# A kernel of attention and feed-forward: one PSUM copy between the two moved from VectorE to ScalarE

## The chip, the cores and the metric

The kernel runs on one Trainium2 chip, on all 8 of its cores. Each core computes one of eight independent batch entries with the same program; nothing is exchanged. The metric is the device time of the slowest core in microseconds. The engines are called PE (TensorE), DVE (VectorE), ACT (ScalarE), POOL (GpSimd) and SP (the one that here issues the output transfers).

## The reference

One layer with a normalisation before and after each half, on x of 8 x 2048 x 1024 (a core has 2048 x 1024):

```
def _layernorm(x, axis=-1, eps=1e-5):
    m = jnp.mean(x, axis=axis, keepdims=True)
    v = jnp.var(x, axis=axis, keepdims=True)
    return (x - m) / jnp.sqrt(v + eps)
...
    x = x + _layernorm(_L0_attn_ref(_layernorm(x, axis=-1), ...), axis=-1)
    x = x + _layernorm(_L0_ffn_ref(_layernorm(x, axis=-1), ...), axis=-1)
```

The attention has 16 heads of 64 and is causal; the feed-forward has 3072 hidden units, silu(gate) * up, with integer weights scaled by 1/127.

## The kernel before

Data lie in SBUF either token-major (128 tokens in the partitions, 1024 features along a row: a tile; there are NJ = 16 tiles) or feature-major (`s_f`, 8 blocks of 128 features by 2048 tokens). Matrix products work on the feature-major form, normalisations on the token-major one. The kernel goes through six stages one after the other: normalise x and transpose it; attention; the output projection (into `s_f`, ACT adds the bias, L750); the stage of this case; the feed-forward; and a last normalisation with the output.

The stage of this case is a software pipeline over the 16 tiles, from the projection's result to the feed-forward's input. For tile j:

- `p3_A(j)`: PE transposes the 8 blocks of the tile from `s_f` into a PSUM bank of `pO` (L762, banks alternate by j % 2); one copy brings the 1024 bf16 values of each partition into `s_ln` as `ztm` (L769, two buffers by j % 2); then `emit_ln` normalises `ztm` into `s_at`.
- `p3_B(j)`: POOL adds the result to the residual `s_x` (L781).
- `p3_C(j)`: `emit_ln` normalises the new `s_x` tile, its mean being known already.
- `p3_D(j)`: PE transposes it into another PSUM bank (L801), and ACT copies that into `s_f` (L809).

`emit_ln` is a chain over two engines: on DVE the sum (L240, left out in `p3_C`), the sum of squares (L246, which reads the tile twice and leaves its product in `s_dmp`), and two small instructions for the variance (L251, L254); on ACT Ln and Exp for the reciprocal root (L257, L260); on DVE one small instruction (L263); on ACT the normalisation itself (L266).

The loop emits step t as

```python
    for t in range(NJ + 3):
        if t < NJ:
            p3_A(t)
        if 0 <= t - 1 < NJ:
            p3_B(t - 1)
        if 0 <= t - 2 < NJ:
            p3_C(t - 2)
        if 0 <= t - 3 < NJ:
            p3_D(t - 3)
```

There is no planner and no reordering: `Prog.op` records each operation with what it reads and writes, and `emit_all` writes them to each engine's queue in the order of emission, with a semaphore wait for each operation that it depends on. An engine works through its queue in that order. So in step t ACT has, of this stage, Ln, Exp and L266 of tile t, then Ln, Exp and L266 of tile t-2, then L809 of tile t-3.

The last stage (`p6_T`, `p6_L`, `p6_AD`) has a similar pipeline, where ACT copies the transposed tile out of PSUM into `s_ln` (L917).

Of the kernel before, what the change touches and what calls it, by code (L numbers as in the profile page):

```python
# [26 lines left out]
class Prog:  # L27
# [12 lines left out]
    def op(self, engine, emit, reads=(), writes=(), queue=None, war=(),  # L40
           deps=(), bump=()):
        idx = len(self.ops)
        dep = set(deps)
        for r in reads:
            e = self.res.get(r)
            if e is not None and e[0] is not None:
                dep.add(e[0])
        for w in tuple(writes) + tuple(war):
            e = self.res.get(w)
            if e is not None:  # L50
                if e[0] is not None:
                    dep.add(e[0])
                dep |= e[1]
        dep.discard(idx)
        self.ops.append({"engine": engine, "emit": emit, "deps": dep,
                         "queue": queue, "token": None})
        for r in reads:
            self.res.setdefault(r, [None, set()])[1].add(idx)
        for w in writes:
            self.res[w] = [idx, set()]  # L60
        for w in bump:
            self.res.setdefault(w, [None, set()])[0] = idx
        return idx
# [59 lines left out]
def build_program(trunc=0, trunc_step=None):  # L123
# [40 lines left out]
    op = P.op  # L164
# [591 lines left out]
    def p3_A(j):  # L756
        par = j % 2
        bank1 = "ps%d" % (4 + par)
        pb = pO[:, 512 * par:512 * (par + 1)].bitcast(BF16)
        for c in range(ND):  # L760
            op("pe",
               lambda e, c=c, j=j, pb=pb: e.transpose(  # L762
                   pb[:, 128 * c:128 * (c + 1)],
                   s_f[:, S * c + 128 * j: S * c + 128 * (j + 1)], IDT),
               reads=["zf_%d_%d" % (c, j // 4), "cst"],
               writes=([bank1] if c == 0 else []),
               bump=([] if c == 0 else [bank1]))
        ztm = s_ln[:, 1024 * par:1024 * (par + 1)]
        op("dve", lambda e, pb=pb, ztm=ztm: e.tensor_copy(ztm, pb[:, 0:1024]),  # L769
           reads=[bank1], writes=["lnr%d" % par],  # L770
           war=["osc0", "osc1"])
        yn = s_at[:, 1024 * par:1024 * (par + 1)]
        emit_ln(ztm, "lnr%d" % par, yn, "yn%d" % par, pid=j % 4, eng="dve",
                dst_war=("at0",) if j < 2 else (),
                war0=(["rrq0", "rrq1", "onq0", "onq1"] if j == 0 else ()))
# [37 lines left out]
# [9 lines that stand above are left out]
# [169 lines left out]
```

How the kernel before makes its waits and increments, by code:

```python
        def body(ename, eng):  # L89
            wm = {}
            def wait(ch, val):
                if wm.get(ch, 0) < val:
                    eng.wait_ge(sems[ch], val)
                    wm[ch] = val
            for i in per_eng[ename]:
                o = ops[i]
                if o["queue"] is not None and i in burst_settle:
                    wait(o["queue"], burst_settle[i])
                for d in sorted(o["deps"]):
                    ch, val, _ = ops[d]["token"]
                    if ops[d]["queue"] is not None:
                        val = burst_end_val[d]
                    wait(ch, val)
                inst = o["emit"](eng)
                if o["token"] is not None:
                    ch, val, inc = o["token"]
                    inst.then_inc(sems[ch], inc)
            if ename == "sp":
                for d in sorted(final_deps):
                    ch, val, _ = ops[d]["token"]
                    wait(ch, val)
```

## Time and profile before

| | us |
|---|---|
| median of the runs | 1687.67 |
| the profiled execution | 1688.74 |
| its span, first to last instruction of the slowest core | 1687.2 |
| spans of the eight cores in it | 1680.3 to 1687.2 |

The profiled execution's time is that of the whole launch; the span leaves out what lies around the first and last instruction of the slowest core (core 2, from which all rows are). A row of the timeline gives the start and the duration in microseconds, counted from the start of the span; in brackets stands how long the engine had been idle before it and which instruction ended the wait. PEld is PE's weight load. In a name like `s_ln<-pO` the left side is written and the right side read. The stage of this case lies between about 981 and 1101 us.

### The profile page before, as it was taken

The page shows a single profiled execution, that of the slowest core. Times are in us where ns is not written, and L with a number is a line of the kernel's source. Part 1 is how long each engine was busy: PE and PEld are TensorE (multiplying, and loading weights), DVE is VectorE, ACT ScalarE, POOL GpSimd, SP SyncE. Part 2 cuts the span into 40 slices and gives each one's busy share as a digit, 9 for nine tenths or more (in the row PEclk, how much of TensorE's full clock was granted, in tenths as well). Part 3 has the DMA queues.
Part 4 walks back from the last instruction along what each step waited for, and adds up shares of the span by engine and source line. Part 5 has one row for each costly group of instructions (what it writes and reads, how often), then busy time and mean ns, then how long its engine had stood idle before and what let it go on. Part 6 is the DMA issues. An engine that isn't in the chain of part 4 may idle for free.

```text
span 1687.2 us, 22074 instructions; the slowest of 8 cores (1680.3 to 1687.2 us)
## 1 busy us (share of the span) xinstructions
PE 1210.9 (72%) x5544; PEld 539.4 (32%) x5648; DVE 503.4 (30%) x1074; ACT 668.8 (40%) x1004; POOL 222.0 (13%) x197
## 2 busy tenths in 40 slices
PE   1437676676767767667776942299999999999920
PEld 0113232232323323222222422144444444444410
DVE  4553233231322313233121057711111211000076
ACT  3243554645455463454656335621111111011154
POOL 5202101010010101001000123311111111000022
PEclk9768798897978979798787965589999999999955
DMA  7401100001010010000000300044333335333122
GB/s 86 55 1 19 13 14 7 10 11 13 13 14 10 4 17 10 1 5 9 10 4 7 32 6 1 4 44 42 38 39 38 38 38 53 30 38 38 19 88 112
DMA packets 114632, 43.49 MB, mean 26 GB/s; under 512 B 109264, under 2 KB 109392, under 8 KB 114512
## 3 DMA queue, kind: packets, MB, share of 16 engines
q0 software_dynamic: 110208, 31.46, 18.5%
q1 hardware_dynamic: 3584, 10.49, 1.8%
q8 instruction: 52, 0.85, 0.2%
q14 instruction: 68, 0.56, 0.1%
q10 hardware_dynamic: 720, 0.13, 0.0%
HBM read 63.05 MB, written 8.39 MB: 42 GB/s over the span
## 4 chain that ended last, share of the span: by engine, by line
PE 63%; DVE 17%; ACT 10%; issue 7%; DMA 1%; POOL 0%; DVEq 0%; ACTq 0%; POOLq 0%
PE pS L841 10%; PE pO L852 10%; PE pS L887 10%; PE pS L624 7%; PE pS L378 7%; PE pO L561 7%; DVE s_dmp L246 5%; ACT s_at L647 5%; PE pS L453 3%; PE pS L316 3%; DVE s_dmp L240 3%; ACT s_dmp L510 2%; ACT pO L506 1%; DVE s_at L462 1%; DVE s_b L391 1%
## 5 line engine op out<-in xcount | busy, mean ns | idle before, releaser
L647 ACT ACTIVATE s_at<-pS,s_nB 128x512 bf16<-128x512 f32 (+4 forms) x521 | 349.2, 707 | 312.8 <-PE pS L632 157.6
L624 PE MATMUL pS<-s_b,s_y 128*128 128x512 bf16 (+3 forms) x622 | 221.0, 399 | 31.5 <-ACT s_at L647 14.4
L561 PE MATMUL pO<-s_at,s_b 128*128 128x512 bf16 (+3 forms) x628 | 192.0, 404 | 14.7 <-ACT s_at L647 7.0
L841 PE MATMUL pS<-s_f,s_wb 128*128 128x512 bf16 x752 | 181.4, 381 | 1.0 <-issue 0.2
L852 PE MATMUL pO<-s_f,s_wb 128*128 128x512 bf16 x753 | 180.5, 380 | 0.8
L887 PE MATMUL pS<-s_b,s_wd 128*128 128x512 bf16 x752 | 165.1, 379 | 0.8
L861 ACT ACTIVATE s_dmp<-pS 128x512 bf16<-128x512 f32 x96 | 57.3, 597 | 270.6 <-PE pS L841 270.6
L866 DVE TENSOR_TENSOR s_b<-s_dmp,pO 128x512 bf16<-128x512 bf16 x96 | 66.0, 688 | 271.1 <-PE pO L852 264.8
L378 PE MATMUL pS<-s_f,s_wb 128*128 128x512 bf16 x373 | 121.2, 425 | 20.3 <-ACT s_f L292 10.3
L330 POOL TENSOR_TENSOR s_wd<-s_b 128x512 bf16<-128x512 bf16 x64 | 66.6, 1040 | 405.8 <-DVE s_b L391 365.1
L624 PEld LDWEIGHTS pS<-s_b,s_y 128*128 128x128 bf16 x640 | 69.5, 110 | 126.0 <-issue 91.0
L841 PEld LDWEIGHTS pS<-s_f,s_wb 128*128 128x128 bf16 x768 | 75.5, 98 | 91.4 <-issue 1.7
L852 PEld LDWEIGHTS pO<-s_f,s_wb 128*128 128x128 bf16 x768 | 75.4, 98 | 91.3 <-issue 1.3
L887 PEld LDWEIGHTS pS<-s_b,s_wd 128*128 128x128 bf16 x768 | 75.1, 98 | 90.6
L502 DVE CAST s_ln<-pO 64x1024 bf16<-64x1024 f32 x32 | 38.9, 1216 | 195.4 <-PE pO L561 195.2
L561 PEld LDWEIGHTS pO<-s_at,s_b 128*128 128x128 bf16 x640 | 61.1, 106 | 109.3 <-issue 79.0
L240 DVE TENSOR_SCALAR_CACHE_REDUCE s_dmp<-s_ln 128x1024 bf16<-128x1024 bf16 x32 | 38.9, 1216 | 168.5 <-ACT s_ln L917 166.6
L515 PE MATMUL pO<-s_dmp,s_cst 1*64 1x512 bf16 x32 | 16.1, 504 | 88.7 <-ACT s_dmp L510 88.7
L801 PE MATMUL pO<-s_cst,s_at 128*128 128x128 bf16 x128 | 16.2, 306 | 86.9 <-ACT s_at L266 86.9
L896 ACT ACTIVATE s_f<-pS 128x512 bf16<-128x512 f32 x32 | 19.1, 597 | 148.4 <-PE pS L887 148.4
L632 PE MATMUL pS<-s_cst 128*128 128x128 bf16 x256 | 63.4, 248 | 0.7 <-ACT s_at L647 0.4
L284 PE MATMUL pO<-s_cst,s_ln 128*128 128x128 bf16 x128 | 15.0, 290 | 64.9 <-ACT s_ln L266 64.9
(90 smaller groups left out, 1226.8 us busy)
## 6 DMA issues: line engine op xcount, KB each, us to landing
y<-s_y SPq DMA_DIRECT2D x16, 512.0 KB, 2.6
s_wb<-wg POOLq DMA_DIRECT2D x24, 256.0 KB, 4.4
s_wb<-wu POOLq DMA_DIRECT2D x24, 256.0 KB, 4.4
s_wd<-wd POOLq DMA_DIRECT2D x8, 768.0 KB, 9.7
s_x<-x POOLq DMA_DIRECT2D x16, 256.0 KB, 7.3
s_wb<-wq POOLq DMA_DIRECT2D x8, 256.0 KB, 4.5
s_b<-s_dmp SPq DMA_DIRECT2D x16, 128.0 KB, 2.2
s_wb<-wo POOLq DMA_DIRECT2D x8, 256.0 KB, 4.5
```

What stands on the lines that cost most here:

```text
L240: op("dve", lambda e, mc=mc: e.tensor_scalar(dmp, src_ap, 1.0 / D, 0.0, ALU.mult, ALU.add, accum_out=mc), reads=[src_res], writes=[mres, " ...
L246: op("dve", lambda e: e.scalar_tensor_tensor(dmp, src_ap, 1.0 / D, src_ap, ALU.mult, ALU.mult, accum_out=cell(3)), reads=[src_res], writes ...
L330: op("pool", lambda e, src_ap=src_ap, q2=q2: e.tensor_mul(q2, src_ap, src_ap), reads=[dres], writes=["q2%d" % par])
L378: e.matmul(out, wslot(slot)[:, 128 * kc:128 * (kc + 1)], xfm(kc)[:, 512 * si:512 * (si + 1)], start=first, stop=(kc == ND - 1), skip_group ...
L561: e.matmul(pO[:, q0:q0 + n], s_b[:, V0 + 1040 * j + 65 * h: V0 + 1040 * j + 65 * h + 128], s_at[:, 2048 * par + (q0 - 128 * j): 2048 * par ...
L624: e.matmul(pS[:, 512 * sl:512 * sl + n], kpadv[hp][:, 128 * ktc:128 * (ktc + 1)], q_fm(c)[:, q0:q0 + n], start=True, stop=(not diag), skip ...
L632: lambda e, sl=sl: e.matmul(pS[:, 512 * sl:512 * sl + 128], NEGI, LMSK, start=False, stop=True, skip_group_check=True),
L647: lambda e, src=src, dst=dst, c=c: e.activation(dst, src, AF.Exp, bias=s_nB[:, c:c + 1], scale=QSCALE),
L841: e.matmul(acc_view(si), wslot(gslot)[:, 128 * kc:128 * (kc + 1)], xfm(kc)[:, 512 * si:512 * (si + 1)], start=first, stop=(kc == ND - 1)),
L852: e.matmul(pO[:, 512 * si:512 * (si + 1)], wslot(uslot)[:, 128 * kc:128 * (kc + 1)], xfm(kc)[:, 512 * si:512 * (si + 1)], start=first, sto ...
L866: lambda e, hc=hc, si=si, stg=stg: e.tensor_tensor(s_b[:, S * hc + 512 * si: S * hc + 512 * (si + 1)], stg, pO[:, 512 * si:512 * (si + 1)] ...
L887: e.matmul(acc_view(si), s_wd[:, 3072 * slot + 128 * hc: 3072 * slot + 128 * (hc + 1)], s_b[:, S * hc + 512 * si: S * hc + 512 * (si + 1)] ...
```

## The change

The copy of `ztm` out of PSUM is issued by ACT instead of DVE. Its source, its destination, its place in the program and what it depends on stay the same; nothing else is edited.

```diff
@@ -766,7 +766,7 @@
                writes=([bank1] if c == 0 else []),
                bump=([] if c == 0 else [bank1]))
         ztm = s_ln[:, 1024 * par:1024 * (par + 1)]
-        op("dve", lambda e, pb=pb, ztm=ztm: e.tensor_copy(ztm, pb[:, 0:1024]),
+        op("act", lambda e, pb=pb, ztm=ztm: e.copy(ztm, pb[:, 0:1024]),
            reads=[bank1], writes=["lnr%d" % par],
            war=["osc0", "osc1"])
         yn = s_at[:, 1024 * par:1024 * (par + 1)]
```

## Rows read from the trace of the kernel before

**Rows 1.** The page's first table: busy time, share of the span, instructions.
```profile
PE 1210.9 (72%) x5544; PEld 539.4 (32%) x5648; DVE 503.4 (30%) x1074; ACT 668.8 (40%) x1004; POOL 222.0 (13%) x197
```

**Rows 2.** The instructions of L769: ns minimum/median/maximum, first and last start.
```profile
L769 DVE COPY s_ln<-pO x16: 680/681/692, 981.6 to 1085.3; 128x1024 bf16<-128x1024 bf16 x16
```

**Rows 3.** Windows: length, busy of PE, PEld, DVE, ACT, POOL; PEclk, DMA share, GB/s.
```profile
1020.00:1040.00 20.00, 5.60 (x48) 4.88 (x48) 14.71 (x38) 11.90 (x21) 6.36 (x3) 0.50 0.00 0
```

**Rows 4.** Timeline of all engines in the stage, one steady period.
```profile
1001.41 1.22 DVE L240 TENSOR_SCALAR_CACHE_REDUCE s_dmp<-s_ln 128x1024 bf16<-128x1024 bf16 x1
...
1014.53 0.21 DVE L263 TENSOR_SCALAR s_st<-s_sx,s_st 128x1 f32<-128x1 f32 x1 [0.70 <-ACT s_st L260]
1014.66 0.68 DVE L769 COPY s_ln<-pO 128x1024 bf16<-128x1024 bf16 x1
1014.84 1.24 ACT L266 ACTIVATE s_at<-s_x,s_st 128x1024 bf16<-128x1024 bf16 x1 [0.41 <-DVE s_st L263]
1015.47 1.22 DVE L240 TENSOR_SCALAR_CACHE_REDUCE s_dmp<-s_ln 128x1024 bf16<-128x1024 bf16 x1
1015.99 0.99 ACT L809 COPY s_f<-pO 128x1024 bf16<-128x1024 bf16 x1
...
1016.80 1.23 DVE L246 SCALAR_TENSOR_TENSOR s_dmp<-s_ln 128x1024 bf16<-128x1024 bf16 x1
...
1017.03 1.06 PE L762 MATMUL pO<-s_cst,s_f 128*128 128x128 bf16 x8
...
1018.52 0.20 ACT L257 ACTIVATE s_st<-s_st 128x1 f32<-128x1 f32 x1 [1.54 <-DVE s_st L254]
...
1019.25 1.21 DVE L246 SCALAR_TENSOR_TENSOR s_dmp<-s_x 128x1024 bf16<-128x1024 bf16 x1
...
1020.81 2.12 POOL L781 TENSOR_TENSOR s_x<-s_x,s_at 128x1024 bf16<-128x1024 bf16 x1 [4.91 <-ACT s_at L266]
...
1021.56 0.21 DVE L263 TENSOR_SCALAR s_st<-s_sx,s_st 128x1 f32<-128x1 f32 x1 [0.70 <-ACT s_st L260]
1021.69 0.68 DVE L769 COPY s_ln<-pO 128x1024 bf16<-128x1024 bf16 x1
...
1022.49 1.22 DVE L240 TENSOR_SCALAR_CACHE_REDUCE s_dmp<-s_ln 128x1024 bf16<-128x1024 bf16 x1
```

**Rows 5.** Timeline of the stage's start, tiles 0 to 2.
```profile
981.14 0.69 ACT L750 ACTIVATE s_f<-pS,s_bo 128x512 bf16<-128x512 f32 x1 [1.04 <-PE pO L762]
...
982.41 1.22 DVE L240 TENSOR_SCALAR_CACHE_REDUCE s_dmp<-s_ln 128x1024 bf16<-128x1024 bf16 x1
...
986.06 0.21 DVE L263 TENSOR_SCALAR s_st<-s_st 128x1 f32<-128x1 f32 x1 [0.70 <-ACT s_st L260]
...
986.99 1.22 DVE L240 TENSOR_SCALAR_CACHE_REDUCE s_dmp<-s_ln 128x1024 bf16<-128x1024 bf16 x1
...
987.76 2.11 POOL L781 TENSOR_TENSOR s_x<-s_x,s_at 128x1024 bf16<-128x1024 bf16 x1 [18.76 <-ACT s_at L266]
...
988.33 2.63 DVE L246 SCALAR_TENSOR_TENSOR s_dmp<-s_ln 128x1024 bf16<-128x1024 bf16 x1
...
992.98 1.22 DVE L240 TENSOR_SCALAR_CACHE_REDUCE s_dmp<-s_ln 128x1024 bf16<-128x1024 bf16 x1
```

**Rows 6.** Timeline of the last stage, where ACT makes the copy L917.
```profile
1601.46 1.92 ACT L917 COPY s_ln<-pO 128x1024 bf16<-128x1024 bf16 x2
1602.59 1.22 DVE L240 TENSOR_SCALAR_CACHE_REDUCE s_dmp<-s_ln 128x1024 bf16<-128x1024 bf16 x1 [166.61 <-ACT s_ln L917]
...
1607.83 1.24 ACT L266 ACTIVATE s_y<-s_ln,s_st 128x1024 f32<-128x1024 bf16 x1 [0.41 <-DVE s_st L263]
...
1609.21 1.01 ACT L917 COPY s_ln<-pO 128x1024 bf16<-128x1024 bf16 x1
```

**Rows 7.** Timeline of the stage's end: L240 of tile 15, the feed-forward's first weight load.
```profile
1086.09 1.22 DVE L240 TENSOR_SCALAR_CACHE_REDUCE s_dmp<-s_ln 128x1024 bf16<-128x1024 bf16 x1
...
1101.07 0.25 PEld L841 LDWEIGHTS pS<-s_f,s_wb 128*128 128x128 bf16 x2
```

## Prediction

> **What bounds the kernel now.** I read the page's header first [rows 1]: over the whole span DVE is busy 30% and ACT 40%, so by the averages nothing here hangs on DVE. But the edit touches only 16 instructions, so the whole-span shares decide nothing. The one line that changes, L769, tells where to look [rows 2]: 16 copies of 0.68 us, from 981.6 to 1085.3 us, all in the stretch between the output projection and the feed-forward. The table by windows [rows 3] shows that stretch: in 20 us DVE works 14.7, ACT 11.9, PE 5.6 and POOL 6.4. PE has almost nothing to do there, so its granted clock (0.50, the 1.2 GHz level) doesn't matter. DVE is the busiest and still idles 5.3 us in 20.
>
> Why it idles is in the timeline of one steady period [rows 4]. I call the tile whose copy runs t. DVE's queue holds: copy(t), L240(t), L246(t), L251 and L254(t), L263(t), then L246(t-2), L251, L254, L263(t-2). ACT's holds: Ln, Exp and Identity (L266) of t, the same three of t-2, then L809, the copy of the normalised tile t-3 into s_f. Each L263 on DVE waits for Ln and Exp on ACT, which wait for DVE's L254. So the stage is one chain that goes back and forth, and a period is its length: L240 starts at 1001.41 and, twelve tiles on, at 1086.09 [rows 4, 7], 7.06 us per tile; the shown one takes 1022.49-1015.47 = 7.02. (Twelve times 7.02 is 84.2, the twelve together take 84.7: an odd 0.4 us lies among them.)
>
> The piece that matters is the handover from one tile to the next: L263(t-2) starts at 1014.53, the copy at 1014.66, L240 at 1015.47 [rows 4]. That is 0.94 us, of which 0.80 is the copy with its gap. At the same time ACT is busy: L266(t-2) starts at 1014.84, L809 at 1015.99. Today these two run in the shadow of DVE.
>
> **What the change does, part by part.** It takes 16 copies off DVE (16 x 0.80 = 12.8 us of chain) and puts 16 on ACT. Their place in ACT's queue is given by the order of emission: the copy of tile t+1 is emitted after everything of step t, so it stands behind L266(t-2) and L809(t-3). An engine works in order, so the first DVE instruction of the next tile, L240, now waits for three ACT instructions in a row. That is where the gain turns into a wait.
>
> Price of one ACT copy: no L769 on ACT exists, but L917 is the same form (128x1024 bf16 out of PSUM into s_ln, on ACT) and takes 1.01 us (1609.21 in [rows 6]), against 0.68 on DVE [rows 2]. No table load shows between the L809 copies and the Ln and Exp around them, so I add none.
>
> The Trainium skill, page "ScalarE: Activation LUTs", section "Rules for kernel authors", speaks against this change: cheap elementwise work belongs on VectorE. The trace agrees on the direction, 0.68 against 1.01. The same page's "What ACT_TABLE_LOAD costs" would make such a copy an estimated 186 + 0.833 x 1024 = 1039 ns; by that the sum below would be 0.4 us more.
>
> New handover, step by step:
> - L263(t-2) start to L266(t-2) start: 1014.84-1014.53 = 0.31.
> - L266 to L809: 1015.99-1014.84 = 1.15. (L266 itself is 1.24 long; neighbours on ACT overlap by 0.09.)
> - L809 to the new copy: 0.99-0.09 = 0.90. The two back-to-back copies of L917 say the same: 1.92 for both less 1.01 is 0.91 [rows 6].
> - the copy 1.01, and 0.12 from its end to L240: the first of the two L917 ends at 1601.46+0.91+0.10 = 1602.47, and L240 starts at 1602.59 [rows 6].
>
> Sum 3.49 us, against 0.94 before: **+2.55 us per tile**. The rest of the period, L240(t) to L263(t-2) = 1021.56-1015.47 = 6.09, stays. New period 9.58 us. Nothing else becomes later: PE's transposes for the next tile begin at 1017.03 and the copy today comes at 1021.69, 3.6 us after they end. POOL's addition runs from 1020.81 to 1022.93, after L246(t-2) (1019.25 to 1020.46) and before the next L246 (1.33 after L240, as 1016.80 is); the new order moves that next one further away.
>
> Which handovers pay it: L809 stands in the queue from step 3 on, so 3→4 to 14→15, twelve of them: 12 x 2.55 = **30.6**. The start, from [rows 5]:
> - tile 0: the last L750 starts on ACT at 981.14 and the copy may follow 0.69-0.09 = 0.60 later; then 1.01 and 0.12: L240 at 982.87 instead of 982.41, **+0.46**.
> - 0→1: no L809 yet, so 0.31+1.15+1.01+0.12 = 2.59 instead of 986.99-986.06 = 0.93, **+1.66**.
> - 1→2 takes 992.98-986.99 = 5.99 today, with an L246 of 2.63 us instead of 1.23. It coincides with POOL's addition (987.76 to 989.87) and ends 1.09 after it. Once L240 of tile 1 comes 3.65 (986.06-982.41) + 2.59 = 6.24 after tile 0's, that L246 starts at 7.57 after it, the addition being over at 7.46. So it takes 1.23, and the step takes 6.24: **+0.25**.
> - 2→3 takes 1001.41-992.98 = 8.43 today, with the same long L246, and 6.09+2.59 = 8.68 then: **+0.25**.
>
> The Trainium skill, page "SBUF — State Buffer", section "SBUF: two separate sides", says that GpSimd and a DVE instruction with two SBUF inputs take a shared port pair by exclusive lock, the later one blocking until the earlier is done. L246 has two SBUF inputs, and the 2.63 in [rows 5] agrees. Without such a lock the two long ones would stay and the sum would be 2.8 larger (a rival below).
>
> The tail doesn't change: after L240 of tile 15 (1086.09) no copy is left, and the feed-forward's first weight load at 1101.07 [rows 7] moves with the chain. From there PE is the bound and takes the shift over in full. Sum: 30.6 + 0.46 + 1.66 + 0.25 + 0.25 = **33.2 us**. The profiled execution took 1688.74 (span 1687.2) and would be 1721.9; the median of the runs is 1.07 lower, so I forecast 1687.67 + 33.2 = **1720.9 us**, 1.97% slower.
>
> **The rivals.**
> 1. *DVE is relieved and ACT hides the copy* (the other side). Then 16 x 0.80 = 12.8 us go: 1674.9. For it: ACT idles 1.54 us before L257 at 1018.52 [rows 4], and the transposes end at 1018.09. It decides if the copy can start by about 1020.5, 1.1 us ahead of the L263(t-2) start at 1021.56. Against it: the order of emission puts the copy behind L266(t-2), which starts after that L263. Chance 0.04.
> 2. *L809 does not stand before the copy on the chain* (it comes late enough to be passed, or costs less than its time). Then each handover is 2.59: 12 x 1.65 + 2.6 = 22.4, 1710.1. Against: L809's input was ready long before, and it follows L266 without a gap. Chance 0.03.
> 3. *ACT's neighbours don't overlap once the copy stands there.* L266 to L917 is 1609.21-1607.83 = 1.38 in [rows 6], 0.23 more than 1.15; there the copy overwrites what that very L266 reads. Here it overwrites what an L266 two tiles older read. If one of the two seams opens, 12 x 0.23 = +2.8: 1723.7; if both, 1726.4. Chance 0.08.
> 4. *The long L246 at tiles 1 and 2 have another cause and stay*: +2.8, 1723.7. Against: the shown one ends 1.09 after POOL's addition, as if it had waited for it, and where no addition is in the way (1016.80, 1019.25) L246 takes 1.2. Chance 0.03.
>
> **How the numbers follow.** The forecast has 0.81. Its own error: each handover step is read to 0.01 to 0.03 us, times twelve 0.1 to 0.4 each; the odd 0.4 us may fall into an idle stretch; execution to execution some 0.1% (1.1 us between the profiled time and the median here). That makes its own range 1718 to 1724. To take in rival 3 at both seams and a slightly shorter handover, the range is 1717 to 1727; rivals 1 and 2 (0.07) stay outside. 2% (about what a measurement of this kernel can tell from no change) is 33.8 us, 1721.4: just 0.5 above the forecast. So the forecast's 0.81 is split 0.46 within and 0.35 beyond, and rivals 1 and 2 both end within 2%: 0.46+0.07 = 0.53. Slower has 0.35+0.08+0.03 = 0.46. The 0.01 that no case holds goes to faster, for which I see no mechanism.
>
> **What would show it.** In the new profile: the period of L240 in the stage 9.6 us (7.0: rival 1; 8.7: rival 2; 9.8 or more: rival 3); DVE idle before L240 about 3.3 us per tile, released by the copy on ACT; ACT's row of L266, L809, copy without gaps; 1.2 us for each L246 of tiles 1 and 2 (rival 4: 2.6). The feed-forward should start 33 us later and last as long. The prediction is wrong if ACT gets to the copy before L809, or if the time moves outside this stage.

## The result, and the profile after

The changed kernel takes 1722.0 us (median of 8 runs, 1721.34 to 1722.86), the kernel before 1687.99 us in the same comparison. The ratio is 1.0203, 95% interval 1.0191 to 1.0215: about 34 us slower. That is 1.1 us above the forecast of 1720.9 and inside the range of 1717 to 1727 (0.3 of the 1.1 is the kernel before, which the forecast had at 1687.67); the interval lies across the 2% line on which the forecast had sat. (In some runs, here two of the eight of the kernel before, the cores of one die or of both show a lower clock; the ratios leave these out, the medians do not.)

The page's first table of the changed kernel answers to [rows 1]. ACT has 13.7 us more, DVE 10.2 less, and none of it explains 34:

```profile
PE 1220.2 (71%) x5648; PEld 539.5 (31%) x5648; DVE 493.2 (29%) x1058; ACT 682.5 (40%) x1020; POOL 221.7 (13%) x197
```

The copies themselves (answer to [rows 2], slowest core, which is now core 3), first and last start, and who waited for them:

```profile
L769 ACT COPY s_ln<-pO x16: 988/1011/1013, 980.7 to 1119.0; 128x1024 bf16<-128x1024 bf16 x16
...
  DVE s_dmp L240: 104.7, 16
```

All 16 are now waited for by L240. (Of the 104.7 us, 58.55 are DVE's idle time during the projection, ahead of tile 0; the rest is 46.) One handover in the timeline of all engines, answer to [rows 4]:

```profile
1008.96 0.21 DVE L263 TENSOR_SCALAR s_st<-s_sx,s_st 128x1 f32<-128x1 f32 x1 [0.70 <-ACT s_st L260]
1009.27 1.24 ACT L266 ACTIVATE s_at<-s_x,s_st 128x1024 bf16<-128x1024 bf16 x1 [0.41 <-DVE s_st L263]
1010.42 0.99 ACT L809 COPY s_f<-pO 128x1024 bf16<-128x1024 bf16 x1
...
1011.31 1.01 ACT L769 COPY s_ln<-pO 128x1024 bf16<-128x1024 bf16 x1
...
1012.44 1.22 DVE L240 TENSOR_SCALAR_CACHE_REDUCE s_dmp<-s_ln 128x1024 bf16<-128x1024 bf16 x1 [3.26 <-ACT s_ln L769]
```

ACT goes through L266, L809 and the copy without a gap, and DVE stands still for 3.26 us in front of L240. The handover is 3.48 us, where it was 0.94. The stretch from L240 of tile 3 to L240 of tile 15, by windows, columns as in [rows 3]:

```profile
1002.87:1120.08 117.21, 22.51 (x194) 19.39 (x191) 57.05 (x144) 61.21 (x96) 25.38 (x12) 0.50 0.00 1
```

It took 84.68 before [rows 4, 7] and takes 117.21 now. The whole stage, from the last L750 to the first L841, went from 119.93 to 154.98 us, 35.05 more. The spans differ by 33.2 (1687.2 and 1720.4), because the core shown now enters the stage 1.06 us earlier (last L750 at 980.08, before 981.14) and what follows the stage is 0.8 us shorter; where cores enter it varies by some 7 us in either profile (974.4 to 981.1 before, 973.4 to 980.1 after).

The twelve periods are not alike. L240 starts at 1002.87, 1012.44, 1022.29, 1031.86, then every 9.57 up to 1089.30, and then at 1100.94: one period of 9.85 and one of 11.64. The long one, tile 12:

```profile
1092.95 0.21 DVE L263 TENSOR_SCALAR s_st<-s_st 128x1 f32<-128x1 f32 x1 [0.70 <-ACT s_st L260]
1093.26 1.24 ACT L266 ACTIVATE s_at<-s_ln,s_st 128x1024 bf16<-128x1024 bf16 x1 [0.41 <-DVE s_st L263]
1093.41 1.23 DVE L246 SCALAR_TENSOR_TENSOR s_dmp<-s_x 128x1024 bf16<-128x1024 bf16 x1 [0.24 <-issue]
...
1094.64 2.11 POOL L781 TENSOR_TENSOR s_x<-s_x,s_at 128x1024 bf16<-128x1024 bf16 x1 [7.45 <-ACT s_at L266]
1094.87 1.90 DVE L254 TENSOR_TENSOR s_st<-s_st 128x1 f32<-128x1 f32 x1
```

L246 comes 0.33 us late (0.46 after L263 instead of 0.13) though it waits for nothing that the profile shows. L254, one column wide and 0.16 us long everywhere else in the stage, therefore starts after POOL's addition instead of just before it, and takes 1.90 us: it ends at 1096.77, POOL's addition at 1096.75. All eight cores show this period.

In the kernel before, the L254 of tile t-2 starts 0.11 us ahead of POOL's addition, which comes at 1020.81 in [rows 4]; and one L254 there, of tile 11, is late by 0.36 us without colliding with anything:

```profile
1020.70 0.16 DVE L254 TENSOR_TENSOR s_st<-s_st 128x1 f32<-128x1 f32 x1
...
1060.77 0.16 DVE L254 TENSOR_TENSOR s_st<-s_st 128x1 f32<-128x1 f32 x1 [0.46 <-DVE s_st L251]
```

In the period of 9.85 us of the changed kernel it is an ACT instruction, Ln, that is late, by 0.28 us (idle 3.45 us before it instead of 3.17):

```profile
1015.77 0.20 ACT L257 ACTIVATE s_st<-s_st 128x1 f32<-128x1 f32 x1 [3.45 <-DVE s_st L254]
```

### The profile page after: what moved, and what is told of

Read it like the earlier page. It is cut to its first block, busy times and chain, and to the rows that moved or that the text cites. A ratio compares the mean times of both kernels' runs of the same rounds, so it can differ in the third digit from the quotient of the medians.

```text
span 1720.4 us, 22126 instructions; the slowest of 8 cores (1713.2 to 1720.4 us)
## 1 busy us (share of the span) xinstructions
PE 1220.2 (71%) x5648; PEld 539.5 (31%) x5648; DVE 493.2 (29%) x1058; ACT 682.5 (40%) x1020; POOL 221.7 (13%) x197
## 4 chain that ended last, share of the span: by engine, by line
PE 62%; DVE 16%; ACT 12%; issue 8%; DMA 1%; POOL 0%; DVEq 0%; ACTq 0%; POOLq 0%
PE pS L841 10%; PE pO L852 10%; PE pS L887 10%; PE pS L624 8%; PE pS L378 7%; PE pO L561 7%; DVE s_dmp L246 5%; ACT s_at L647 5%; PE pS L316 3%; PE pS L453 3%; DVE s_dmp L240 3%; ACT s_dmp L510 1%; ACT pO L506 1%; DVE s_at L462 1%; DVE s_b L391 1%
## 5 line engine op out<-in xcount | busy, mean ns | idle before, releaser
L624 PE MATMUL pS<-s_b,s_y 128*128 128x512 bf16 (+3 forms) x640 | 228.2, 402 | 29.9 <-ACT s_at L647 13.4
L841 PE MATMUL pS<-s_f,s_wb 128*128 128x512 bf16 x768 | 183.2, 382 | 0.0
L378 PE MATMUL pS<-s_f,s_wb 128*128 128x512 bf16 x384 | 124.4, 427 | 18.5 <-ACT s_f L292 10.6
L240 DVE TENSOR_SCALAR_CACHE_REDUCE s_dmp<-s_ln 128x1024 bf16<-128x1024 bf16 x32 | 38.9, 1216 | 271.4 <-ACT s_ln L917 166.6
L841 PEld LDWEIGHTS pS<-s_f,s_wb 128*128 128x128 bf16 x768 | 75.5, 98 | 91.3 <-issue 1.6
L801 PE MATMUL pO<-s_cst,s_at 128*128 128x128 bf16 x128 | 16.2, 306 | 119.9 <-ACT s_at L266 119.9
L257 ACT ACTIVATE s_st<-s_st 128x1 f32<-128x1 f32 x64 | 13.0, 203 | 135.1 <-DVE s_st L254 135.1
```

What stands on the lines that cost most here:

```text
L240: op("dve", lambda e, mc=mc: e.tensor_scalar(dmp, src_ap, 1.0 / D, 0.0, ALU.mult, ALU.add, accum_out=mc), reads=[src_res], writes=[mres, " ...
L378: e.matmul(out, wslot(slot)[:, 128 * kc:128 * (kc + 1)], xfm(kc)[:, 512 * si:512 * (si + 1)], start=first, stop=(kc == ND - 1), skip_group ...
L624: e.matmul(pS[:, 512 * sl:512 * sl + n], kpadv[hp][:, 128 * ktc:128 * (ktc + 1)], q_fm(c)[:, q0:q0 + n], start=True, stop=(not diag), skip ...
L841: e.matmul(acc_view(si), wslot(gslot)[:, 128 * kc:128 * (kc + 1)], xfm(kc)[:, 512 * si:512 * (si + 1)], start=first, stop=(kc == ND - 1)),
```

## The experiments

The theory: the cost is the place of the copy in ACT's queue. What stands there between L263(t-2) and L240(t+1) is paid in full for each tile, and what stands elsewhere costs nothing. The main rival: ACT's copy costs as work, being longer (1.01 us against 0.68) and loading ACT with 16 us more, wherever it stands. A second question is what makes the period of 11.64 us.

**The same instructions, the copy a tile ahead.** `p3_A` is split into transposes with copy, and the normalisation (`p3_AL`):

```diff
-    for t in range(NJ + 3):
-        if t < NJ:
-            p3_A(t)
+    p3_A(0)
+    for t in range(NJ + 3):
+        if t + 1 < NJ:
+            p3_A(t + 1)
+        if t < NJ:
+            p3_AL(t)
```

> The changed kernel, with the transposes and the ACT copy of tile t+1 emitted before the normalisation of tile t, so that in ACT's queue the copy stands ahead of Ln(t), where ACT idled 1.5 us before the change. Same instructions, same engines, another order. Theory (the order costs, because the copy stood behind L266 and L809 on the chain): the handover L263(t-2) to L240(t+1) falls from 3.48 to 0.13 us, ACT comes about 0.1 us late to Ln, so the period is 6.3 us instead of 9.57; tiles 0 to 2 gain about 5 us more because POOL's addition no longer catches L246. Sum against the kernel before: +0.5 - 0.8 - 2.2 - 2.1 - 12 x 0.71 - 0.4 = -13.5, about 1674.5. Rival (the ACT copy costs because it is 1.01 us instead of 0.68 and loads ACT with 16 us more, wherever it stands): stays near 1722, in any case above the kernel before.

Measured: 1676.72 us beside 1686.87 of the kernel before, ratio 0.9939 (0.9926 to 0.9952). With the copy on ACT and nothing changed but the order, the kernel is 10 us faster than the one before, where the changed kernel is 34 slower. The rival that the copy costs as work is out. One period, core 2 (L805 and L813 are L801 and L809, moved by four lines):

```profile
1023.88 1.21 DVE L240 TENSOR_SCALAR_CACHE_REDUCE s_dmp<-s_ln 128x1024 bf16<-128x1024 bf16 x1
1024.06 1.24 ACT L266 ACTIVATE s_at<-s_x,s_st 128x1024 bf16<-128x1024 bf16 x1 [0.42 <-DVE s_st L263]
...
1025.20 0.99 ACT L813 COPY s_f<-pO 128x1024 bf16<-128x1024 bf16 x1
...
1026.10 1.01 ACT L769 COPY s_ln<-pO 128x1024 bf16<-128x1024 bf16 x1
...
1027.00 0.21 ACT L257 ACTIVATE s_st<-s_st 128x1 f32<-128x1 f32 x1
...
1030.18 1.21 DVE L240 TENSOR_SCALAR_CACHE_REDUCE s_dmp<-s_ln 128x1024 bf16<-128x1024 bf16 x1
```

ACT does the same three in a row, but L240 has started before them; the period is 6.30 us, as expected (6.3). I had expected 13.5 us of gain and got 10.2. The miss is at tiles 1 and 2, where I had counted a gain of 4.3: there L246 holds POOL's addition up (2.96 us instead of 2.12), and then L254 is shut out, that is, it can't finish before the addition does:

```profile
986.92 1.23 DVE L246 SCALAR_TENSOR_TENSOR s_dmp<-s_ln 128x1024 bf16<-128x1024 bf16 x1
...
987.17 2.96 POOL L785 TENSOR_TENSOR s_x<-s_x,s_at 128x1024 bf16<-128x1024 bf16 x1 [19.39 <-ACT s_at L266]
...
988.39 1.75 DVE L254 TENSOR_TENSOR s_st<-s_st 128x1 f32<-128x1 f32 x1
```

Twice 1.59 us (1.75 less 0.16) is 3.2, of a miss of 3.3.

**The same order with the copy on DVE.** The edit is the one above, with `op("dve", ... tensor_copy` for the copy.

> The kernel before (copy on DVE) with the same order as the run with the copy a tile ahead: DVE copies tile t+1 before L240 of tile t. It tells whether the order alone brings something. Theory: DVE still does the same work in its chain, 0.80 us per copy, so the period stays 7.03 and the time within 2 us of the kernel before, 1688. Rival (the early emission itself is what helps, by freeing PE or by another overlap): about as much faster as the ACT version, 1675.

Measured: 1683.32 beside 1686.87, ratio 0.9978 (0.9968 to 0.9987). Neither fits well: I had expected no change within 2 us, and it is 3.7 faster; the rival wanted 12. The order alone brings a third of what order and engine bring together. The trace tells where it comes from (core 0):

```profile
1023.66 0.68 DVE L769 COPY s_ln<-pO 128x1024 bf16<-128x1024 bf16 x1
...
1024.26 1.21 DVE L240 TENSOR_SCALAR_CACHE_REDUCE s_dmp<-s_ln 128x1024 bf16<-128x1024 bf16 x1
```

From the copy to L240 it is 0.60 us, where it was 0.80 to 0.81 in the kernel before [rows 4]. L240 no longer reads what the copy just wrote. The semaphore wait (L94) that the program puts between the two for that reason is gone, and L240 starts before the copy has ended. The period is 6.81 instead of 7.03. So of the 0.80 us per tile, 0.20 was the wait of an instruction for its neighbour's result; how much of that is the wait instruction itself was not tried.

**L809 behind the copy.** Only the two ACT copies change places.

```diff
-    for t in range(NJ + 3):
+    for t in range(NJ + 4):
         if t < NJ:
             p3_A(t)
+        if 0 <= t - 4 < NJ:
+            p3_D(t - 4)
+        if t < NJ:
+            p3_AL(t)
...
-        if 0 <= t - 3 < NJ:
-            p3_D(t - 3)
```

> The changed kernel with L809 of tile t-3 emitted one place later, behind the copy of tile t+1 and ahead of Ln(t+1). Same instructions on the same engines; only these two copies change places on ACT. Theory: the handover is 0.31 + 1.15 + 1.01 + 0.11 = 2.57 us instead of 3.48 at twelve handovers, 12 x 0.91 = 10.9 us less: 1711.1, or 1709 if the single long period at tile 12 goes too. Rival (ACT's load or the slower copy costs, not the order): unchanged at 1722.

Measured: ratio 1.0141 (1.0122 to 1.0161), which is 1710.7 beside 1686.87; the profiled execution took 1710.24. The forecast was 1711.1. The period is 8.66 us:

```profile
1042.92 0.21 DVE L263 TENSOR_SCALAR s_st<-s_sx,s_st 128x1 f32<-128x1 f32 x1 [0.70 <-ACT s_st L260]
1043.23 1.24 ACT L266 ACTIVATE s_at<-s_x,s_st 128x1024 bf16<-128x1024 bf16 x1 [0.41 <-DVE s_st L263]
1044.38 0.99 ACT L769 COPY s_ln<-pO 128x1024 bf16<-128x1024 bf16 x1
...
1045.27 1.01 ACT L813 COPY s_f<-pO 128x1024 bf16<-128x1024 bf16 x1
1045.49 1.22 DVE L240 TENSOR_SCALAR_CACHE_REDUCE s_dmp<-s_ln 128x1024 bf16<-128x1024 bf16 x1 [2.35 <-ACT s_ln L769]
```

The handover is 2.57 and DVE idles 2.35 instead of 3.26. L809 is as long as before and runs beside L240 now. The ratio rests on two runs only, but the trace agrees: the stage, from the last L750 to the first L841, is 11.05 us shorter than in the changed kernel (143.97 instead of 155.02, medians of the cores), 10.9 expected. The long period at tile 12 stays, 10.73 us.

**A second ACT copy, ahead of the first and behind it.** Both kernels make a further copy of the same PSUM bank into SBUF that is free at that time, so they do work that the result doesn't need.

```diff
+        dum = s_y2[:, 1024:1536].bitcast(BF16)
+        op("act", lambda e, pb=pb, dum=dum: e.copy(dum, pb[:, 0:1024]),
+           reads=[bank1], writes=["dum"], war=["kp1", "kpz1"])
         op("act", lambda e, pb=pb, ztm=ztm: e.copy(ztm, pb[:, 0:1024]),
...
```

This is the copy ahead; the other kernel has the same three lines behind the copy of `ztm`. In both, one more line makes the last stage wait before it uses that memory.

> The changed kernel with a second ACT copy of each tile's PSUM bank into unused SBUF, emitted just ahead of the copy of ztm, so that it stands on the handover. It adds work and leaves the output as it is. Theory (what stands in ACT's queue between L263(t-2) and L240(t+1) is paid in full): 0.90 us more for each of 16 tiles, handover 4.4 instead of 3.48, +14.4 us: 1736.4 where the changed kernel has 1722. Rival (ACT's total load decides): +14.4 too, here and in the run with the second copy behind.

> As the run with the second copy ahead, but the second copy is emitted just behind the copy of ztm, ahead of Ln. The same 16 extra ACT instructions. Theory: L240 starts when the first copy is done, and ACT idles 3.17 us before Ln, so the 0.90 us are hidden: unchanged at 1722, within 1 us (2 us if the one long period moves). Rival (ACT's total load decides): +14.4, about 1736.

Measured beside 1687.51: ahead 1736.29, ratio 1.0289 (1.0271 to 1.0307); behind 1721.68, ratio 1.0208 (1.0188 to 1.0228). The forecasts were 1736.4 and 1722. The same 16 instructions cost 14 us in front of the copy and nothing behind it; the stage alone takes 169.33 and 154.68 us, where the changed kernel has 155.02 (medians of the cores). The idle time of ACT ahead of Ln takes them in; first the row of the changed kernel:

```profile
1005.92 0.20 ACT L257 ACTIVATE s_st<-s_st 128x1 f32<-128x1 f32 x1 [3.17 <-DVE s_st L254]
```

and then of the kernel with the second copy (into `s_y`) behind, core 1, where that idle time is 0.92 less and L240 still starts 0.12 after the end of the first copy:

```profile
1029.77 1.01 ACT L769 COPY s_ln<-pO 128x1024 bf16<-128x1024 bf16 x1
1030.68 1.02 ACT L773 COPY s_y<-pO 128x1024 bf16<-128x1024 bf16 x1
1030.90 1.22 DVE L240 TENSOR_SCALAR_CACHE_REDUCE s_dmp<-s_ln 128x1024 bf16<-128x1024 bf16 x1 [3.26 <-ACT s_ln L769]
...
1033.95 0.20 ACT L257 ACTIVATE s_st<-s_st 128x1 f32<-128x1 f32 x1 [2.25 <-DVE s_st L254]
```

In both kernels the period of 9.85 us is gone, while the long one of tile 12 stays (12.57 and 11.65 us). Only ACT's queue has more instructions here, not DVE's.

**Twelve small DVE instructions ahead of the stage.** Now to the 11.64 us period.

```diff
+    for k in range(12):
+        cl = 16 * (k // 6) + 8 + k % 6
+        op("dve", lambda e, cl=cl: e.memset(s_st[:, cl:cl + 1], 0.0))
```

> The changed kernel with 12 one-column memsets put into DVE's queue before the stage, while DVE idles there. The trace of the changed kernel has one period of 11.64 us (tile 12) instead of 9.57: L246 comes 0.33 us late with nothing to wait for, so that L254 of tile 10 starts 0.23 us after POOL's addition and takes 1.90 us instead of 0.16. In the kernel before DVE stands still for 0.36 us at the same ordinal of its queue (row 1467 in both), where it hits L254 of tile 11 and collides with nothing. Theory: the pause belongs to a place in the instruction stream, and the collision to where that place falls; the 12 fillers move it back onto L254 of tile 11. Expected: no L254 above 0.2 us, one period of 9.9 instead of 11.6, total 1.7 us less, about 1720.3. Rival (the pause or the long L254 comes from the moment or the data, not from the place in the queue): the 11.6 us period stays at tile 12, 1722.

Measured: median 1718.84 beside 1686.87, 32.0 more, where the changed kernel has 34.0 more; the interval of the ratio (1.0175 to 1.0245) is too wide to settle 2 us, so the trace has to. In it no L254 of the stage is longer than 0.16 us, and L240 of tiles 12 and 13 start 9.57 us apart (1085.99 and 1095.56 on core 0); the stage takes 152.88 us instead of 155.02 (medians of the cores), 2.14 less. The long period is gone, without a wait or a dependence of the stage being touched. One thing came out differently: I had expected the pause to hit L254 of tile 11 again, and it is nowhere to be seen. Counted in DVE's queue from 0 and with its semaphore instructions, row 1467 is L254 of tile 11 in the kernel before and the wait in front of the late L246 in the changed one; in the kernel with the fillers it is the wait in front of L240 of tile 12, where DVE idles 3.26 us anyway. My expectation had the count wrong: each copy had a semaphore wait of its own, so the twelve copies ahead of that place took 24 rows with them, and twelve fillers bring back half (L254 of tile 11 is row 1467, then 1443, then 1455). In the copy-ahead kernel the late instruction is again at row 1467. The pause belongs to the place in the instruction stream, and its price to what stands there: 0.36 us, 2.07 us, or nothing.

The traces show more than was tried. The place is not the only one: DVE also pauses at row 1339 where the copy ahead is made by DVE (0.35 us, in front of L263), and ACT's late Ln is row 2491 of ACT's queue in the changed kernel; in the kernel before a pause of 0.28 us falls on that row too, where it costs nothing. ACT shows another at row 2619. These rows are 128 apart, 1339 to 1467 and 2491 to 2619, and at each of the four a packet of 8192 bytes of an instruction queue starts 1.0 to 1.4 us after the start of the row ahead, on all eight cores of the kernel before, the changed kernel and the one with the fillers, also where the pause is hidden. That points to the loading of instructions as the cause; no run varied it, so it is not shown.

**L254 with one tensor input.** Is it the two SBUF inputs of L254 that shut it out?

```diff
-        op("dve", lambda e: e.tensor_tensor(s_st[:, b + 4:b + 5], cell(3),
-                                            cell(4), ALU.subtract),
+        op("dve", lambda e: e.tensor_scalar(s_st[:, b + 4:b + 5], cell(3),
+                                            cell(4), None, ALU.subtract),
```

> The changed kernel with L254, the subtraction of two one-column cells, written as a tensor_scalar (one tensor, the other cell as a scalar) instead of a tensor_tensor. Theory (the 1.90 us of L254 at tile 12 is a tensor instruction with two SBUF inputs shut out while POOL adds): with one tensor input it isn't shut out; it takes 0.21 us everywhere, as L251 does, also where the 0.33 us pause lets it start after POOL's addition, so the 11.6 us period becomes 9.9 to 10.0. The 32 uses in the stage lie on the chain and cost 0.05 us each, 1.5 in all, so the total hardly moves: 1722 - 1.7 + 1.5, about 1722. Rival (the L254 waits for something else, as a late semaphore): a long one stays at tile 12.

Measured: 1722.97 beside 1687.51, ratio 1.0213 (1.0193 to 1.0233), no different from the changed kernel, as expected. The trace decides (core 2, tile 12):

```profile
1094.38 1.23 DVE L246 SCALAR_TENSOR_TENSOR s_dmp<-s_x 128x1024 bf16<-128x1024 bf16 x1 [0.24 <-issue]
...
1095.61 2.11 POOL L781 TENSOR_TENSOR s_x<-s_x,s_at 128x1024 bf16<-128x1024 bf16 x1 [7.57 <-ACT s_at L266]
...
1095.84 0.21 DVE L254 TENSOR_SCALAR s_st<-s_st 128x1 f32<-128x1 f32 x1
```

The same pause, the same late start, 0.23 us into POOL's addition, and it takes 0.21 us. On core 0 that period is 10.03 us instead of 11.64 and the others are 9.69 instead of 9.57, which eats the gain. The subtraction still reads a second cell of SBUF, as the scalar, so what counts here is the second tensor input.

**A faster version that fell short.** With the copy ahead, DVE still idles 0.79 and 0.70 us per period in front of the two L263. Here `emit_ln` is cut in three (the sum; the squares up to Exp; L263 and L266) and the parts are spread over the loop:

```diff
-    for t in range(NJ + 3):
+    p3_A(0)
+    for t in range(NJ + 4):
         if t < NJ:
-            p3_A(t)
...
+            p3_AL(t, 0)
+        if 0 <= t - 3 < NJ:
+            p3_C(t - 3, 2)
+        if t < NJ:
+            p3_AL(t, 1)
+        if t + 1 < NJ:
+            p3_A(t + 1)
         if 0 <= t - 2 < NJ:
-            p3_C(t - 2)
...
+            p3_C(t - 2, 1)
+        if 0 <= t - 4 < NJ:
+            p3_D(t - 4)
+        if t < NJ:
+            p3_AL(t, 2)
+            p3_B(t)
```

> The ACT copy a tile ahead, and emit_ln in three parts spread over the loop, so that DVE has an L240 or an L246 to do while ACT makes Ln and Exp: L263 and L266 of tile t-3's second normalisation come after L240 of tile t, L263 of tile t after L246 of tile t-2. Same instructions. In the copy-ahead run DVE idles 0.79 and 0.70 us per period of 6.30 before the two L263. Theory: both waits are covered, and ACT (about 5.5 us of work and gaps) or POOL's lock against L246 sets the period at 5.6 to 6.0: 14 x 0.5 = 7 us less than the copy-ahead run (1676.7 beside 1686.9 before), about 1670. Rival (the chain is already limited by ACT and POOL at 6.3): no gain, 1677, or a loss where L246 and POOL's addition meet in each period.

Measured: 1680.58 beside 1687.51, ratio 0.9959 (0.9944 to 0.9975): faster than before, but not than the copy ahead alone (0.9939; the intervals overlap, and the traces settle it: the stage takes 111.99 us here and 109.69 there, medians of the cores). The rival holds, in its second form, a loss where DVE and POOL's addition meet. Most periods are 6.44 us on core 5, with this in them (L258, L250 and L792 are L254, L246 and L781):

```profile
1044.55 2.12 POOL L792 TENSOR_TENSOR s_x<-s_x,s_at 128x1024 bf16<-128x1024 bf16 x1 [4.32 <-ACT s_at L271]
1044.66 2.03 DVE L258 TENSOR_TENSOR s_st<-s_st 128x1 f32<-128x1 f32 x1
```

Is it that L254 alone, or the lock as such?

> The interleaved kernel (1680.6) with L254 as a tensor_scalar with one tensor input, as in the run that showed it immune to POOL's addition. In the interleaved kernel L254 is shut out in each period for 2.04 us. Theory (the lock sets the period, and it holds for the next L246 as well): L254 is 0.21 again, but the L246 behind it, with two tensor inputs, still cannot start before the addition ends; only Ln and Exp of the tile come earlier. No gain: 1680.6 within 1.5 us. Rival (the shut-out L254 alone is what made interleaving slower than the copy ahead alone): period 5.6 to 6.0, about 1670.

Measured: 1682.33 beside 1688.29, ratio 0.9963 (0.9948 to 0.9979). No gain. L254 is 0.21 us again, and L246 behind it is shut out in its place (core 5), with most periods at 6.43 us:

```profile
1028.69 2.12 POOL L792 TENSOR_TENSOR s_x<-s_x,s_at 128x1024 bf16<-128x1024 bf16 x1 [4.31 <-ACT s_at L271]
1028.74 0.21 DVE L258 TENSOR_SCALAR s_st<-s_st 128x1 f32<-128x1 f32 x1
1028.88 3.02 DVE L250 SCALAR_TENSOR_TENSOR s_dmp<-s_x 128x1024 bf16<-128x1024 bf16 x1
```

**Both small gains together**, the copy ahead and L254 with one input:

> The copy-ahead kernel (1676.7 beside 1686.9) with L254 as a tensor_scalar with one tensor input. There two L254, of tiles 1 and 2, take 1.75 us because POOL adds. Theory: both fall to 0.21, 3.1 us less, and the 32 uses in the stage cost 0.05 us each more, 1.5: 1.6 us less, ratio 0.993 to the kernel before. Rival (what L254 waited for just moves to the next L246): no gain or 1.5 us slower.

Measured: 1676.50 beside 1688.29, ratio 0.9934 (0.9918 to 0.9949), against 0.9939 (0.9926 to 0.9952) without the L254 edit. The intervals overlap, so the gain is not shown by the times; in the traces L240 of tile 15 comes 91.47 us after that of tile 0, where it was 92.99 (core 0 in both), beside the 1.6 expected.

## Why the prediction was right, and where it was not exact

*What bounds the kernel.* Right: the stage is one chain over DVE and ACT. With the same instructions on the same engines, the order of two ACT copies moves the time by 10.5 us (ratio 1.0141 instead of 1.0203), and emitting the copy a tile ahead by 44 (0.9939).

*Price of one ACT copy, 1.01 us from L917.* Measured 1.01 (0.99 in some). No table load appeared in the stage.

*The handover of 3.49 us.* Measured 3.48, with the same parts: 0.31, 1.15, 0.89, and 1.13 from the copy's start to L240. The period of 9.58 is 9.57. Rival 3, gaps between ACT's neighbours, didn't come. Nor did rival 1, for the reason given (the order of emission); the run with the copy ahead shows what it is worth when the order allows it: 10 us less than the kernel before, where rival 1 had 12.8. Rival 2's handover of 2.59 was made by the run with L809 behind: 2.57 measured.

*The start.* L750 to L240 of tile 0 went from 1.27 to 1.70 us, +0.43 (said: 0.46). Tile 0 to 1 takes 6.22 (6.24), 1 to 2 takes 6.21 (6.24), 2 to 3 takes 8.66 (8.68). L246 of tiles 1 and 2 is 1.23 us, as it had to be if the 2.63 came from POOL's addition (rival 4 is out). The Trainium skill's rule on the shared port pair ("SBUF — State Buffer", section "SBUF: two separate sides") agrees with that, and with L254 as a subtraction of two tensors; that a cell of SBUF read as the scalar does not count as such an input is what the run with the one-input L254 shows.

*The twelve handovers, 30.6 us.* Measured 117.21 - 84.68 = 32.53. The mis-sized term is what I called "an odd 0.4 us". I let it vanish or stay, and had no reason why it could not grow. It is a pause at a fixed place in DVE's queue. The change takes twelve copies with their waits, 24 rows, out of that queue ahead of this place and so moves the pause from one L254 to the gap between an L263 and an L246. ACT, and with it POOL, had been released by that L263 and did not wait; the pause became a collision and costs 2.07 us instead of 0.36. The pause of 0.28 us on ACT (L257 at 1015.77, 0.37 after L254's end instead of 0.10) cost nothing before and now stands on the chain. 2.07 + 0.28 - 0.36 = 1.99, beside the difference of 1.93 between 32.53 and 30.6. The fillers took the first away, and with it 2.14 us of the stage. The margin of 0.11 us stood plainly in the profile before, in each period. I had looked only at the L246 beside it.

*The total.* It came closer than its parts, and that was luck. The stage grew by 35.05 us where the forecast had 33.2, and what follows it, from the first L841 on, was 0.8 us shorter (585.20 instead of 585.98, medians of the cores), where the forecast had it unchanged. That remainder lies between 584.6 and 586.0 us in the profiles of kernels with the same code behind the stage, so a difference of this size also stands between kernels that differ only in the stage.

*The 2% line.* The forecast was 1.97%, the result 2.03% with an interval that covers both sides. The 2.0 us of the two pauses are 0.12%, enough to carry it across.

## What to carry to other kernels

An engine's free time can only take over work where the queue has it: before moving an instruction, look at what stands in front of it in its new queue and who waits behind, and count all of that, not the instruction's own length. If the data are ready earlier, emit the moved instruction earlier; here the same sixteen copies on ACT are worth +34 us in one place and -10 us in another. And a small two-input DVE instruction that starts 0.1 us ahead of a POOL operation in each period is a trap for the next edit: here a change in the number of instructions ahead of it was enough, since it moved a pause to just in front of it.

## What the runs showed of the hardware that I had not expected

- DVE pauses for 0.33 to 0.36 us at row 1467 of its queue (semaphore instructions counted, from 0), on all cores, with nothing to wait for in the profile. It stays at that row when 24 rows are removed ahead of it or 12 put back; what it costs was 0.36, 2.07 or 0 us. ACT pauses for 0.28 us at row 2491 of its own. A further pause of either engine lies 128 rows from these, and at each of these rows an 8192-byte packet of an instruction queue starts within 1.0 to 1.4 us of the row ahead; that the loading is the cause was not tried.
- A one-column L254 was shut out by POOL's addition for the whole of it: 1.75 to 2.08 us instead of 0.16, according to when it started. As a tensor_scalar it took 0.21 at the same moment.
- It goes the other way too: where L246 starts first, POOL's addition takes 2.96 us instead of 2.12.
- On DVE a copy of 0.68 us whose result the next instruction reads, with the semaphore wait that the program puts there, costs 0.80 us of the queue, and 0.60 when the next instruction reads something older and has no wait ahead of it.
